# A cross-attention and MX feed-forward layer on one core: first norms of the epilogue taken by halves, and one set of power operations for a gated and a normed tile

## What is computed

```python
x = x + attention(layernorm(x), ctx)         # ends with @ Wp + bp
r = bf16(layernorm(x))                        # "residual"
h = bf16(layernorm(r) * ln_w + ln_b)
h = bf16(mx_quant(h) @ mx_quant(W1).T + b1)   # 512 -> 2048
h = bf16(gelu(h))                             # the "gated" tile, 2048 wide
h = bf16(mx_quant(h) @ mx_quant(W2).T + b2)   # 2048 -> 512
out = x + bf16(r + h)
```

## Time and profile before

| | |
|---|---|
| runs before | 2722.95 us median of 3 (2720.22 to 2727.97) |
| the profiled execution's own time | 2737.58 us |
| its span (all rows below are in it) | 2735.8 us |
| start of the epilogue in the span | 2444.8 us |
| share of the span: PE, DVE, ACT, POOL | 82%, 91%, 72%, 52% |
| mean granted clock of TensorE | 0.821 |

### The profile page before, as it was taken

One profiled execution on the slowest core, in us unless ns is written; L12 is line 12 of the kernel. 1 busy time (PEld: TensorE's weight loads), 2 busy tenths in 40 slices (PEclk: granted clock), 3 DMA queues, 4 the chain that ended last, 5 costly groups with the idle time before them and its releaser, 6 DMA issues. The chain is left out here.

```text
span 2735.8 us, 52956 instructions
## 1 busy us (share of the span) xinstructions
PE 2249.1 (82%) x20003; PEld 1193.3 (44%) x20020; DVE 2492.6 (91%) x3592; ACT 1983.4 (72%) x1813; POOL 1419.5 (52%) x1855
## 2 busy tenths in 40 slices
PE   8899899968888888788888788888887777867886
PEld 4444454424444444444444444444444444433443
DVE  6998667879999999999999999999999999957997
ACT  3344333458888888888888888888988888864665
POOL 2432222136556575666757667675775758552001
PEclk9999999967677777777777876787777888779999
DMA  7565445489999999999999999999999999991000
GB/s 228 123 146 114 89 97 120 90 190 175 197 177 202 203 181 197 181 197 185 191 210 180 193 200 193 192 183 211 178 197 194 189 195 175 180 213 43 16 16 27
DMA packets 1389368, 442.13 MB, mean 162 GB/s; under 512 B 1323924, under 2 KB 1364372, under 8 KB 1387576
## 3 DMA queue, kind: packets, MB, share of 16 engines
q1 hardware_dynamic: 1378472, 397.08, 76.7%
q10 hardware_dynamic: 10736, 43.11, 6.3%
HBM read 78.99 MB, written 42.35 MB: 44 GB/s over the span
## 5 line engine op out<-in xcount | busy, mean ns | idle before, releaser
L888 DVE TENSOR_SCALAR_CACHE_REDUCE arena<-a_ps_s 128x1281 f32<-128x1281 f32 (+1 forms) x1280 | 1826.3, 1488 | 46.1 <-PE a_ps_s L833 38.1
L940 ACT ACTIVATE arena<-arena,a_bias,a_row_scale 128x3328 uint8<-128x3328 f32 (+1 forms) x512 | 1560.4, 3048 | 257.4 <-POOL a_bias L1003 255.7
L833 PE MATMUL a_ps_s<-arena,a_q_rep 96*128 96x512 bf16 (+2 forms) x3840 | 1232.4, 443 | 325.0 <-DVE arena L888 290.7
L846 PEld LDWEIGHTS a_ps_o<-a_v_head,a_nT 128*128 128x128 f16 x13056 | 529.6, 103 | 295.2 <-issue 160.9
L833 PEld LDWEIGHTS a_ps_s<-arena,a_q_rep 96*128 (+1 forms) x3840 | 314.6, 109 | 767.8 <-DVE arena L888 417.8
L1010 POOL CAST a_nT<-arena 128x1664 int16<-128x1664 uint8 x256 | 401.8, 1570 | 352.3 <-DMA arena<-arena 349.5
L846 PE MATMUL a_ps_o<-a_v_head,a_nT 128*128 128x32 f16 x13056 | 518.8, 183 | 43.4 <-POOL a_nT L1011 39.8
L1011 POOL CAST a_nT<-arena 128x1664 int16<-128x1664 uint8 x256 | 402.9, 1574 | 0.0
L358 POOL TENSOR_TENSOR p_rest<-p_kq,p_parts 128x512 f32<-128x512 f32 (+1 forms) x51 | 88.8, 1742 | 317.2 <-ACT p_parts L468 317.2
L999 POOL TENSOR_SCALAR a_row_max<-a_row_max,a_part_max 128x1 f32<-128x1 f32 x256 | 92.2, 360 | 246.6 <-DVE arena L888 229.3
L388 PE MATMUL p_ps_k<-p_wkv,p_ctxT 128*128 128x512 f32 (+1 forms) x408 | 190.3, 611 | 0.0
(11 more groups left out here) (151 smaller groups left out, 1943.0 us busy)
## 6 DMA issues: line engine op xcount, KB each, us to landing
k_parts_transposed<-p_stage SPq DMA_DIRECT2D x25, 768.0 KB, 7.0
p_ctx<-in_ctx_dram SPq DMA_DIRECT2D x25, 512.0 KB, 5.8
arena<-k_parts_transposed ACTq DMA_DIRECT2D x48, 240.1 KB, 4.0
late_values<-arena SPq DMA_DIRECT2D x51, 192.0 KB, 6.9
a_late_v<-late_values ACTq DMA_DIRECT2D x6, 1632.0 KB, 9.6
arena<-in_L_ffn_W_dram SPq DMA_DIRECT2D x8, 1024.0 KB, 8.1
arena<-k_parts_transposed ACTq DMA_DIRECT2D x48, 160.1 KB, 3.8
a_q_rep<-q_transposed ACTq DMA_DIRECT2D x48, 128.0 KB, 5.4
```

Of the source, the lines that this page charges most:

```text
L833: last = nc.tensor.matmul(ps_s[:, b, n0:n0 + w], q, k_parts[0:3 * HD, slot, start[c] + n0:start[c] + n0 + w], start=True, stop=True)
L846: last = nc.tensor.matmul(ps_o[:, u, 0:HD], nT[:, u, j, :], v_head[:, v_slot, j, :], start=(j == 0), stop=(j == KT - 1))
L888: nc.vector.tensor_scalar(s_row[:, u, start[c]:start[c] + size[c]], ps_s[:, (u + c) % 2, 0:size[c]], 1.0, None, ALU.mult, ALU.max, accum_o ...
L940: nc.scalar.activation(out, s_row[:, u, keys_of_half[half]], ACT.Exp, scale=row_scale[:, u, 0:1], bias=bias[:, u:u + 1], accum_out=zsum[:, ...
```

## The change

It is all in `finish`. First, the norms of the first pairs are taken in pieces. A list `norms` counts them: columns 0 and 1 of norm 0 (the first pair's residuals), then columns 2 and 3 of norm 1, then columns 0 and 1 of norm 1, and from norm 2 on all four columns as before. In step -2 DVE runs `small` for norm 0, both `moments_of_residual`, the variance of norm 1's columns 2 and 3, then both `add_projection`, the variance of its columns 0 and 1, and `small` for columns 2 and 3; `small` for columns 0 and 1 follows in step -1 between the two hidden tiles. ACT gets a second `roots` in step -2. In steps up to -1 the projections and moments come after both hidden tiles.

Second, gated tile and hidden tile of the same s are quantised by one function `quantise(t, k, i)`: the gated tile's block maxima, `small` if it is due, the hidden tile's two norm operations and its block maxima, then the three power operations once over 80 blocks, then the gated tile's integers and values, then the hidden tile's. DVE waits for its own `gq_ready` and `hq_ready` at the very end.

```diff
-        floor, exponent = ph.sb("floor", [P, BF]), ph.sb("exponent", [P, BF], I32)
-        power, inverse = ph.sb("power", [P, BF]), ph.sb("inverse", [P, BF])
+        floor, exponent = ph.sb("floor", [P, BF + BC]), ph.sb("exponent", [P, BF + BC], I32)
+        power, inverse = ph.sb("power", [P, BF + BC]), ph.sb("inverse", [P, BF + BC])
...
+        norms = [(0, 0, 2), (1, 2, 4), (1, 0, 2)] + [(i, 0, 4) for i in range(2, PAIRS + 1)]
+        def norms_of(i):
+            return (i, 0, 2) if i < 2 else (i, 0, 4)
...
                 copy_heads(x_tiles[1])
+                if n == -2:
+                    roots(1, 2, 4)
                 copy_gated(g_tiles[0])
...
                 if n + LEAD <= PAIRS:
-                    roots(n + LEAD)
+                    roots(*norms_of(n + LEAD))
...
+            def powers(first, last):
+                p, v, f, e = (ap[:, first:last] for ap in (power, inverse, floor, exponent))
+                steps.then_wait(nc.vector.tensor_tensor(p, p, f, ALU.max))
+                steps.then_wait(nc.vector.tensor_tensor(p.bitcast(I32), p.bitcast(I32), e, ALU.bitwise_and))
+                steps.then_wait(nc.vector.tensor_tensor(v.bitcast(I32), p.bitcast(I32), e, ALU.bitwise_xor))
...
+            def quantise(t, k, i):
+                if t is not None:
+                    largest_of_gated(t)
+                if i is not None:
+                    small(*i)
+                if k is not None:
+                    largest_of_hidden(k)
+                if t is not None or k is not None:
+                    powers(0 if t is not None else BF, BF + BC if k is not None else BF)
+                if t is not None:
+                    gated_integers(t)
+                if k is not None:
+                    hidden_integers(k)
+                if t is not None:
+                    dve.wait_ge(gq_ready, t + 1)
+                if k is not None:
+                    dve.wait_ge(hq_ready, k + 1)
...
                 x_tiles, r_tiles, h_tiles, g_tiles = (tiles_of(n + lead) for lead in (LEAD, 2, 1, 0))
+                earlier = norms_of(n - 1 + LEAD) if 0 <= n - 1 + LEAD <= PAIRS else None
+                if n == -2:
+                    small(*earlier)
+                    for s in range(2):
+                        moments_of_residual(r_tiles[s])
+                    variance(1, 2, 4)
+                    for s in range(2):
+                        add_projection(x_tiles[s])
+                    variance(1, 0, 2)
+                    small(1, 2, 4)
+                    continue
                 for s in range(2):
-                    earlier = n - 1 + LEAD
-                    quantise_gated(g_tiles[s], (lambda: small(earlier)) if s == 0 and 0 <= earlier <= PAIRS else None)
-                    quantise_hidden(h_tiles[s])
+                    quantise(g_tiles[s], h_tiles[s], earlier if s == (1 if n == -1 else 0) else None)
                     round_output(2 * n - 1 + s)
-                    add_projection(x_tiles[s])
-                    moments_of_residual(r_tiles[s])
+                    if n > -1:
+                        add_projection(x_tiles[s])
+                        moments_of_residual(r_tiles[s])
+                if n <= -1:
+                    for s in range(2):
+                        add_projection(x_tiles[s])
+                        moments_of_residual(r_tiles[s])
                 if n + LEAD <= PAIRS:
-                    variance(n + LEAD)
+                    variance(*norms_of(n + LEAD))
```

79 lines of the change are left out of this document (36 added, 43 removed).

## The result

The changed kernel takes 2746.24 us, the median of four runs (2741.65 to 2754.74). The kernel before, run beside it, takes 2724.8 us (2720.22 to 2727.97). The ratio is 1.0084, with a 95% interval of 1.0054 to 1.0113: slower, as forecast, but by some 21 us where 11.5 were forecast, and outside the range of 2724 to 2742.

What follows compares the result with a forecast made beforehand. VectorE was taken to set the epilogue's pace. Terms +4.8, +4.5 and +2.2 gave +11.5 us: profiled 2737.58 becomes 2749.1, put on the median 2722.95 as 2734.5 us (+0.42%); range 2724 to 2742.

Steps and rivals of the forecast that it cites:

- The sharing: Each gated and hidden pair in steps 0 to 6: shared power operations save VectorE 0.6 us, 8.4 us over 14 pairs.
- The order and its ring: Five steps: later gated tile delays TensorE and ScalarE's root, VectorE waits 2.3 us; 31.70 us a step, +4.5 us.
- The sum is 31.70 us a step. Five steps take 158.5.: Length of the chain from gated tile to gated tile in the five steps: 158.5 us in place of 154.0, +4.5.
- The rival of the clock: Steps -2, -1, 5 and 6: longer TensorE waits bring 1.2 GHz, slower still, +16.5 us, 2739.5; chance 15%.
- Step -1 and the first gated tile: Start of epilogue: first hidden copy 2.4 us later, gated tile 2.35 us later by the order; +4.8 us.
- I take 2479.1, which is when it started before: Step -2: start of the first hidden tile on VectorE, unchanged, with up to three operations held up by GpSimd.
- the first norms: Steps -2 and -1: taking the first pairs' norms in pieces brings no gain at the first hidden tile.
- Step 5: Steps without projection, gated tile of step 5 to that of step 6: 30.7 us against 28.46, +2.2 us.
- the end: From the gated tile of step 6 to the end of the span: left as it is, 46.7 us, 0 change.
- VectorE keeps the pace: Rival for the epilogue: the root comes in time, all 14 savings count, -8.4 us, priced at 2714.5; chance 12%.
- TensorE close behind: Rival for the steps: root late, but TensorE takes the second gated tile at once; 30.8 us, +6.3, 2729.3; chance 15%.
- The move to the median: Whole time: profiled execution lay 14.6 us above the runs' median 2722.95, so 2749.1 became 2734.5 us.

Runs made afterwards that it cites:

- run 3: Changed kernel with its new order kept, but three separate power operations for each tile again; 2743.77 us, ratio 1.0070.
- Run 4: Changed kernel with ScalarE taking the root ahead of the output copy of s = 1 from step 0 on; 2735.96 us, ratio 1.0050.
- run 5: Changed kernel with needless bias products added on TensorE in front of its waits for a gated tile; 2735.45 us, ratio 1.0054.
- run 10: Kernel before the change with needless bias products added on TensorE in steps 5 to 7 only; 2720.79 us, ratio 0.9982.
- run 1: Changed kernel with its new first norms, but each tile quantised by itself in the old order; 2724.77 us, ratio 1.0012.
- run 2: Changed kernel with the new shared quantise, but norms and order of steps -3 to -1 as before; 2742.60 us, ratio 1.0067.
- run 8: Kernel of run 7 with each tile quantised by itself in the old order, two sets of power operations; 2720.29 us, ratio 0.9980.
- runs 6 to 10: The first of them: changed kernel with the root early and ScalarE's residuals behind the first gated copies (step -1: first hidden copy); 2725.71 us, ratio 0.9990.
- run 7: Changed kernel with early root, residuals moved behind the first copies, and GpSimd's bias additions for tiles 8 to 15 later; 2721.30 us, ratio 0.9985.
- run 9: Kernel of run 7 with needless bias products on TensorE in step 0 and steps 5 to 7; 2726.52 us, ratio 0.9985.

## Why the prediction was right or wrong

**The sharing: right.** 0.6 us a pair forecast, 0.64 measured; and, as said, none of it arrives while VectorE waits (run 3 loses nothing by giving it up).

**The order and its ring: right in kind and size.** The chain was the one that was named: the gated tile 2.35 us later (11.14 - 8.79, as forecast), TensorE late, the hidden copy, the table, the root, VectorE idle. Run 4 cuts it and the waits go. Its length, 31.70 us a step, is that of the steps without a slow product (31.4 to 31.9), and of all five in run 5; VectorE's wait, forecast at 2.3 us, is 2.34 in step 2. (The two parts given for that wait, 1.5 and 0.9, add up to 2.4; nothing else uses it.)

**The step that failed: "The sum is 31.70 us a step. Five steps take 158.5."** The sum took every part of the ring from rows in which TensorE ran at 2.4 GHz. But the ring itself makes TensorE wait 2.11 us a step for the gated tile where it waited 0.8 to 0.9, and 3.83 in step 0. After three of these five waits it ran part of the product at 1.2 GHz (granted 0.66 to 0.74), and that product is on the ring: 5.19, 4.57 and 5.09 us, together 4.4 us more than before. The measured term was +9.5 in place of +4.5; run 5, at 2.4 GHz throughout, gives +4.9. The rival of the clock had the mechanism, but put it only where a long wait already stood, in steps -2, -1, 5 and 6; the wait in the five steps was not worked out, though one more row of the kernel before would have given it:

```profile
2537.23 1.07 PE L1225 MATMUL f_ps_g<-ident,f_gq 128*128 128x128 bf16 x16 [0.83 <-DVE f_gq L1346]
```

From TensorE's start on the gated tile of s = 1 (2521.46) to the end of its work there it is 14.94 us (2537.23 - 0.83 - 2521.46), and the forecast's own ring has the next gated tile taken 16.95 us after that start: a wait of 2.0 us, measured 2.1. The rival's 2739.5 was nearer, but short too. Of the 7.0 us by which the epilogue's forecast fell short (18.5 for 11.5), 5.0 are in these five steps. Without the 4.6 us of the clock there the median would be some 2741.6, just inside the range; that is an estimate from the result and run 5.

**Step -1 and the first gated tile: +3.9 for +4.8.** The hidden tile was turned by 2481.69 (2481.08 + 0.61), and ScalarE, busy with both residuals from 2482.24, copied it at 2484.14: 2.4 us, the term as forecast. What made it cheaper is that the first hidden tile was ready 1.0 us sooner after the start (37.5 for 38.6), since tile 3's projection ran at full clock (3.67 us for 6.70). That is luck and not the change: run 10, the kernel before up to step 5, had it too, and its first gated tile at 60.0. Against that execution the two of the changed kernel are 5.8 and 5.1 us later, and run 1 is 2.7 us later, for the 2.4 forecast. "I take 2479.1, which is when it started before" failed as a number: it started at 2474.73. But GpSimd's additions then held both of its wide operations, 1.83 and 1.63 us for 0.75, so that of three microseconds' lead one was left. The forecast counted at most three such hits; the rows show six. Its conclusion, no gain from the first norms, holds: run 1 had the first hidden tile done at 36.7 us and run 10, with the old norms, at 36.8.

**Step 5: +3.6 for +2.2, the end +1.5 for 0.** Again the clock: the longest waits are here, 5.97 us in step 5, and the clock of the last 80 us is 0.88 where it was 0.91 over 75. With needless products (run 5) the step is 30.1 us, under the 30.7 of the forecast, and the end 44.7, under the 46.7 of before. So leaving the end as it is was the wrong default where its waits grow too. With products slow at other places from run to run, the size of this part is rougher than that of the five steps.

**The rivals.** VectorE keeps the pace: no, its waits of 1.9 to 3.5 us say it. TensorE close behind: no, it waited for the gated tile in each step.

**The move to the median** put 2734.5 where the sum in the profile was 2749.1; the profiled run after was 2754.74. The two profiled executions lay 14.6 and 8.5 us above their medians, so 6.1 of the 11.7 us by which the median missed are this scatter. Of the 21.4 us between the medians, 18.5 are in the epilogue of the profiled executions, and the rest can't be put down to the change.

What stays open: why the same wait of 2.1 us is followed by a slow stretch in steps 2 and 3 and not in steps 1 and 4 (in run 2 it is steps 1 and 3, in run 3 steps 2 and 4); and the tail of run 8. And no version is shown faster in whole time by more than a measurement tells from no change: runs 6 to 10 lie at 0.9980 to 0.9990. What stands firm are parts of the epilogue: 4.4 us less in the five steps (run 7 against run 8, and against the kernel before), and 1.6 us less from step 5 on (run 10). The whole epilogues of run 7 (5.2 us less than before), run 9 (11.2 less) and run 10 (3.4 less) hold chance as well.

## What to carry to other kernels

When work is reordered on the busiest engine, take the result that gets later and follow it through the other engines until it comes back: the margin there (1.2 us at the root) is what the reordering may cost, and a saving smaller than the excess does not arrive at all. Compare a part only with executions that ran it at the same clock (the same instructions took 61.8 and 60.0 us here). Work out each wait that appears on TensorE, small ones too, and price the products behind it at half clock as well. And look for the chain that lies just beneath the bound (30.8 under 30.8 here, through ScalarE's residuals), since a saving on the bound ends there.

## What had not been expected of the hardware

Of the four waits of 2.1 us that TensorE has in steps 1 to 4 of the changed kernel, two were followed by a product partly at 1.2 GHz (4.53 to 5.09 us for 3.40), in both of its profiled executions, and two also in runs 2 and 3, in other steps; of the waits for a gated tile of 0.8 to 1.5 us in the five steps of the kernel before none was. Work that does nothing gave back 4.6 us of 163.5 there, and 1.6 of the last 75.2 us of the kernel before; in run 9 it gave back nothing in steps 5 to 7.

GpSimd's additions of some 1.2 us each held up VectorE's six small operations on two columns and the two wide ones behind them to 8.4 us, where they take 2.6 without them.
